# Shared-expert down product of a two-layer gated block: seven tiles in three passes of split operands, three of them behind the last expert tile, and ranks in the third chunk

## What is computed

```
t = layernorm(x)                                  # 896 tokens x 512
scores = softmax(t @ gate_w.T)                    # 16 experts
weights, indices = top_k(scores, 2)
y = sum over e of swiglu(t, w1[e], w3[e], w2[e]) * w_e      # inner width 352
z = swiglu(t, sw1, sw3, sw2)                      # shared expert, inner width 704
x = x + tanh(g_ffn[1]) * (y + z)
swiglu(t, a, b, o) = (silu(t @ a.T) * (t @ b.T)) @ o.T
```

## Time and profile before

| what | value |
|---|---|
| median of 3 runs | 979.6 us (975.99 to 981.77) |
| the profiled execution, its own time | 978.74 us |
| its span, first to last instruction | 977.1 us |
| PE busy | 939.0 us, 96% |
| DVE, ACT, POOL busy | 45%, 30%, 8% |
| chain that ended last, share of PE | 89% |
| mean granted TensorE clock | 0.987 of full |

### The profile page before, as it was taken

How to read it: one execution, slowest core, us unless ns; L and a number is a source line. 1 busy time by engine, 2 the same in 40 slices (tenths; PEclk the granted TensorE clock), 3 DMA queues, 4 the chain that set the end, 5 groups by cost and what they waited for, 6 DMA issues and landing times.

```text
span 977.1 us, 17840 instructions
## 1 busy us (share of the span) xinstructions
PE 939.0 (96%) x7481; PEld 713.2 (73%) x7482; DVE 442.6 (45%) x747; ACT 291.5 (30%) x466; POOL 74.8 (8%) x110
## 2 busy tenths in 40 slices
PE   5999999999999999989999999999999999999991
PEld 5878787878888787779999445887896455655550
DVE  6664544545445457862220353796344122222224
ACT  4633333333333334642221121335310022222210
POOL 0000000000000003000000000021005102222211
PEclk9999999999999999989999999999999999999996
DMA  8000010000101011052000302900604318977726
GB/s 335 33 2 33 2 33 2 33 27 9 76 1 34 1 62 49 2 204 120 1 1 3 126 1 68 399 27 17 250 1 153 120 33 301 327 246 247 259 72 224
DMA packets 26773, 96.04 MB, mean 98 GB/s; under 512 B 3282, under 2 KB 4306, under 8 KB 23634
## 3 DMA queue, kind: packets, MB, share of 16 engines
q1 hardware_dynamic: 20354, 72.69, 21.0%
q0 software_dynamic: 6352, 22.35, 6.1%
HBM read 76.37 MB, written 18.66 MB: 97 GB/s over the span
## 4 chain that ended last, share of the span: by engine, by line
PE 89%; DVE 5%; ACT 3%; DMA 2%; issue 1%; SPq 0%; POOL 0%; POOLq 0%; DVEq 0%; ACTq 0%
PE ps L554 18%; PE ps L555 16%; PE ps L556 16%; PE ps L971 10%; PE ps L818 7%; PE ps L981 5%; PE ps L634 4%; PE ps L945 4%; PE ps L617 3%; PE ps L840 1%; PE ps L656 1%; PE ps L962 1%; PE ps L603 1%; PE ps L988 1%; DMA token_rows<-arena,to_row 1%
## 5 line engine op out<-in xcount | busy, mean ns | idle before, releaser
L554 PE MATMUL ps<-arena_r 128*125 128x512 f32 (+1 forms) x416 | 164.1, 395 | 2.9 <-DVE arena_r L1322 2.9
L555 PE MATMUL ps<-arena_r 128*125 128x512 f32 (+1 forms) x416 | 157.2, 378 | 0.0
L556 PE MATMUL ps<-arena_r 128*125 128x512 f32 (+1 forms) x416 | 157.0, 377 | 0.0
L554 PE MATMUL ps<-hT,arena_r 128*128 128x448 f32 (+1 forms) x368 | 136.2, 370 | 2.4 <-DVE arena_r L1341 1.1
L556 PE MATMUL ps<-hT,arena_r 128*128 128x448 f32 (+1 forms) x368 | 134.4, 365 | 0.0
L555 PE MATMUL ps<-hT,arena_r 128*128 128x448 f32 (+1 forms) x368 | 134.4, 365 | 0.0
L971 PE MATMUL ps<-arena 128*128 x336 | 102.9, 459 | 0.0
L1037 ACT ACTIVATE arena<-arena,mbias,mscale 125x448 f32<-125x448 f32 x96 | 66.2, 752 | 101.9 <-DVE arena L1449 101.9
L554 PEld LDWEIGHTS ps<-arena_r 128*125 128x125 f32 (+1 forms) x416 | 78.2, 188 | 20.5 <-issue 3.9
L556 PEld LDWEIGHTS ps<-arena_r 128*125 128x125 f32 (+1 forms) x416 | 78.1, 188 | 13.8
L555 PEld LDWEIGHTS ps<-arena_r 128*125 128x125 f32 (+1 forms) x416 | 78.3, 188 | 10.8
(11 more groups left out here) (208 smaller groups left out, 1119.7 us busy)
## 6 DMA issues: line engine op xcount, KB each, us to landing
arena<-in_e SPq DMA_DIRECT2D x16, 1408.0 KB, 6.6
arena<-in_e SPq DMA_DIRECT2D x16, 512.0 KB, 7.5
sorted_rows<-arena POOLq DMA_DIRECT2D x1, 7453.0 KB, 33.4
land_c<-in_ctx SPq DMA_DIRECT2D x8, 752.0 KB, 4.3
arena<-sorted_rows POOLq DMA_DIRECT2D x21, 257.0 KB, 5.6
land_w<-in_gu SPq DMA_DIRECT2D x8, 512.0 KB, 5.1
arena<-token_rows SPq DMA_DIRECT2D x14, 256.0 KB, 4.4
arena<-in_e SPq DMA_DIRECT2D x16, 192.0 KB, 9.1
```

The source lines that it names most:

```text
L554: mm(into, a[0], w[0], start=i == 0, stop=False)
L555: mm(into, a[0], w[1], start=False, stop=False)
L556: last = mm(into, a[1], w[0], start=False, stop=i == len(operands) - 1)
```

## The change

`BEFORE = 4` token tiles of the shared down product stay ahead of or within the first expert tile (tile 3 in two halves), and tiles 4, 5 and 6 go behind the last expert product. Each tile is formed by three fp32r matmuls per chunk in place of one plain one. For that `sh2` and `hsh[m]` are split: ACT copies the high halves, DVE subtracts the low ones (`shared_low`). ACT also keeps copies of `sh2` high and of part of the low half of chunk 4 for the late tiles, because their first places lie in expert slots. Slot 2 is loaded only when tile 3 is done. The rank matmuls move from ahead of chunk 4 into chunk 2, before its last product; on DVE the tables follow at once, and `shared_hidden(2)` to `(5)` come behind them. POOL may scatter the first choice once `dest_set` is 1, and reads its loop counts before it waits for the last scatter. On DVE the late tiles' `shared_out` stands in the last loop, between the adds of j=1.

```diff
@@ memory
-        sh2 = at(37120, 6, D)
-        hsh = [at(31744 + m * TOK, TOK) for m in range(6)]
+        sh2 = halves(19440, 37120, landing("land_2", 37120, 6 * D), 6, D)
+        A_HL = [A_SH + m * 1024 for m in range(4)] + [22512, A_HT]
...
+        hsh = [halves(31744 + m * TOK, A_HL[m], land_h[m], TOK) for m in range(6)]
+        sh2_kept = at_r(896, 6, D)
+        h4_kept = at_r(3968, TOK - BEFORE * P)
...
-        A_XR = A_SH
+        A_XR = 45824
...
-        SHARED_BANK = (4, 5, 0, 1, 0, 1, 0)
+        SHARED_BANK = (4, 5, 0, 1, 0, 1, 2)
@@ SP
-            for e in range(NSLOT):
-                if e == NSLOT - 1:
-                    sp.wait_ge(ff_mm, MC + 6)
-                load_expert(e)
+            load_expert(0)
+            load_expert(1)
+            sp.wait_ge(ff_mm, MC + 6)
+            load_expert(3)
...
             post(1)
+            sp.wait_ge(sh_copied, 9)
+            sp.wait_ge(y_mm, 3 * NT + BEFORE)
+            load_expert(2)
@@ PE
-                if m == 4:
-                    pe.wait_ge(both_set, 1)
-                    pe.wait_ge(tri_set, 4)
-                    mm(ps[:, 6, 0:RT], lower, both.rearrange("p t e -> p (t e)"), start=True, stop=True)
-                    mm(ps[:, 7, 0:RT], ones, both.rearrange("p t e -> p (t e)"), start=True, stop=True
-                       ).then_inc(rank_mm, 1)
                 gate_up(m, sh13[m], size, 0, 0)
                 gate_up(m, sh13[m], size, 1, 0)
-                if m == 4:
+                if m == 3:
                     pe.wait_ge(rank_sv, 2)
                 gate_up(m, sh13[m], size, 0, 1)
+                if m == 2:
+                    pe.wait_ge(ff_h, MC + 2)
+                    pe.wait_ge(chosen, 2)
+                    pe.wait_ge(tri_set, 4)
+                    mm(ps[:, 2, 0:RT], lower, both.rearrange("p t e -> p (t e)"), start=True, stop=True)
+                    mm(ps[:, 3, 0:RT], ones, both.rearrange("p t e -> p (t e)"), start=True, stop=True
+                       ).then_inc(rank_mm, 1)
                 gate_up(m, sh13[m], size, 1, 1).then_inc(ff_mm, 1)
...
+            def shared_part(t, first, end):
+                if first == 0 and t >= 2:
                     pe.wait_ge(y_sv, 3 * NT + t - 1)
...
+                for m in range(first, end):
+                    z = SH_CHUNKS[m]
+                    if t == 0:
+                        pe.wait_ge(hsh_low, m + 1)
...
+                    mm(into, h[0], w[0], start=m == 0, stop=False)
+                    mm(into, h[0], w[1], start=False, stop=False)
+                    last = mm(into, h[1], w[0], start=False, stop=m == 5)
...
-            for t in range(5):
-                shared_down(t)
+            for t in range(BEFORE - 1):
+                shared_part(t, 0, 6)
...
             rows_T(0)
-            shared_down(5)
+            shared_part(BEFORE - 1, 0, 3)
             up_expert(0)
             rows_T(1)
-            shared_down(6)
+            shared_part(BEFORE - 1, 3, 6)
             hidden_T(0)
...
             hidden_T(last1)
+            pe.wait_ge(sh_copied, 9)
+            shared_part(BEFORE, 0, 1)
             down_expert(last1)
+            shared_part(BEFORE, 1, 6)
+            for t in range(BEFORE + 1, NT):
+                shared_part(t, 0, 6)
@@ ACT
+            act.wait_ge(sh_ld, 32)
+            fn(sh2[0][:, 0:4], sh2[2][:, 0:4], ACT.Copy)
+            fn(sh2[0][0:96, 4:6], sh2[2][0:96, 4:6], ACT.Copy).then_inc(w_high, 1)
...
+                if m == 2:
+                    act.wait_ge(rank_mm, 1)
+                    for bank, counted in ((2, place_), (3, tmp16)):
+                        fn(counted.rearrange("p t e -> p (t e)"), ps[:, bank, 0:RT], ACT.Copy).then_inc(rank_sv, 1)
...
+                act.wait_ge(ff_h, MC + m + 1)
+                fn(hsh[m][0][0:size], hsh[m][2][0:size], ACT.Copy).then_inc(sh_copied, 1)
+
+            fn(sh2_kept[:, 0:4], sh2[0][:, 0:4].bitcast(F32), ACT.Copy).then_inc(sh_copied, 1)
+            fn(sh2_kept[0:96, 4:6], sh2[0][0:96, 4:6].bitcast(F32), ACT.Copy).then_inc(sh_copied, 1)
+            act.wait_ge(hsh_low, 5)
+            fn(h4_kept[0:96], hsh[4][1][0:96, BEFORE * P:TOK].bitcast(F32), ACT.Copy).then_inc(sh_copied, 1)
@@ DVE, ranks
             for t in range(NT):
-                then(v.tensor_tensor(place_[:, t, :], place_[:, t, :], cnt, ALU.add))
+                v.tensor_tensor(place_[:, t, :], place_[:, t, :], cnt, ALU.add)
                 then(v.tensor_tensor(cnt, cnt, tmp16[:, t, :], ALU.add))
@@ DVE, the last loop
             for t in range(NT):
+                if t >= BEFORE:
+                    shared_out(t)
                 dve.wait_ge(back_ld[t][1], 16)
...
                 v.tensor_tensor(x[:, t, :], x[:, t, :], back[t][1], ALU.add).then_inc(out_st, 1)
@@ POOL
-            pool.wait_ge(dest_set, 2)
...
+                pool.wait_ge(dest_set, j + 1)
...
-            pool.wait_ge(scattered, 16 * 2 * NT)
             pool.wait_ge(tables_set, 1)
             last3, last2, last1, tiles = counts(pool)
+            pool.wait_ge(scattered, 16 * 2 * NT)
+            pool.wait_ge(ff_h, MC + 6)
```

More of the change, by code:

```diff
@@ L52 @@
 ROW = D + 2
+BEFORE = 4
 LN_EPS = 1e-5
@@ L237, in flamingo @@
         xgT = at(47616, KC, P)
-        A_XR = A_SH
-        yr = at(A_SH + 2 * ROW, D)
-        A_TO = A_SH + 2 * ROW + D
+        A_XR = 45824
+        yr = at(A_XR + 2 * ROW, D)
+        A_TO = A_XR + 2 * ROW + D
         weight = at(A_TO + 8, 1)
-        back = [[at(31744 + (2 * t + j) * D, D) for j in range(2)] for t in range(NT)]
+        back = [[at(28144 + t * D, D), at(4352 + t * D if t < 5 else 44288 + (t - 5) * D, D)] for t in range(NT)]
         lgT = at(9800, TOK, rows_=2 * NE)
@@ L408, in counts @@
                     for i in range(4)]
-        WEIGHTS = ("wk0a", "wk0b", "wv0", "wkv1a", "wkv1b", "gate", "wo0", "wq1", "wg1", "wo1")
+        WEIGHTS = ("wk0a", "wk0b", "wv0", "wkv1a", "wkv1b", "gate", "wo0", "wq1", "wg1", "wo1", "sh2")
         def nth(name):
@@ L934, in _ @@
                 gate_up(m, sh13[m], size, 1, 1).then_inc(ff_mm, 1)
             pe.wait_ge(ff_h, MC + 5)
-            pe.wait_ge(sh_ld, 32)
-            def shared_down(t):
-                if t >= 2:
+            pe.wait_ge(w_low, nth("sh2"))
+            def shared_part(t, first, end):
+                if first == 0 and t >= 2:
                     pe.wait_ge(y_sv, 3 * NT + t - 1)
-                for m, z in enumerate(SH_CHUNKS):
-                    if t == 0 and m == 5:
-                        pe.wait_ge(ff_h, MC + 6)
-                    last = mm(ps[:, SHARED_BANK[t], :], hsh[m][0:z, t * P:(t + 1) * P], sh2[0:z, m, :],
-                              start=m == 0, stop=m == 5)
-                last.then_inc(y_mm, 1)
@@ L949, in _ @@
-            for t in range(5):
-                shared_down(t)
+                into = ps[:, SHARED_BANK[t], :]
+                for m in range(first, end):
+                    z = SH_CHUNKS[m]
+                    if t == 0:
+                        pe.wait_ge(hsh_low, m + 1)
+                    h, w = ([half[0:z, t * P:(t + 1) * P] for half in hsh[m][:2]],
+                            [half[0:z, m, :] for half in sh2[:2]])
+                    if t >= BEFORE:
+                        w[0] = sh2_kept[0:z, m, :]
+                        if m == 4:
+                            h[1] = h4_kept[0:z, (t - BEFORE) * P:(t - BEFORE + 1) * P]
+                    mm(into, h[0], w[0], start=m == 0, stop=False)
+                    mm(into, h[0], w[1], start=False, stop=False)
+                    last = mm(into, h[1], w[0], start=False, stop=m == 5)
@@ L952, in _ @@
+                if end == 6:
+                    last.then_inc(y_mm, 1)
+            for t in range(BEFORE - 1):
+                shared_part(t, 0, 6)
             pe.wait_ge(tables_set, 1)
@@ L1660, in _, with shared_low @@
             feed_low(MC + 1, sh13[1])
+            dve.wait_ge(w_high, nth("sh2"))
+            v.tensor_tensor(sh2[1][:, 0:4], sh2[2][:, 0:4], sh2[0][:, 0:4].bitcast(F32), ALU.subtract)
+            v.tensor_tensor(sh2[1][0:96, 4:6], sh2[2][0:96, 4:6], sh2[0][0:96, 4:6].bitcast(F32), ALU.subtract
+                            ).then_inc(w_low, 1)
             def shared_hidden(m):
-                hidden(MC + m, m, SH_CHUNKS[m], 1.0, silu1[m % 2], hsh[m])
+                hidden(MC + m, m, SH_CHUNKS[m], 1.0, silu1[m % 2], hsh[m][2])
+            def shared_low(m):
+                z = SH_CHUNKS[m]
+                dve.wait_ge(sh_copied, m + 1)
+                v.tensor_tensor(hsh[m][1][0:z], hsh[m][2][0:z], hsh[m][0][0:z].bitcast(F32), ALU.subtract
+                                ).then_inc(hsh_low, 1)
             dve.wait_ge(lg_mm, 3)
@@ L1682, in _ @@
             shared_hidden(1)
+            shared_low(0)
             then(v.tensor_copy(idxf, idx8[:, :, 0:2]))
@@ L1733, in _ @@
             v.tensor_copy(tile_expert[:], texpf).then_inc(tables_set, 1)
+            shared_hidden(2)
+            shared_low(1)
```

(19 more changed lines are left out.)

42 lines of the change are left out of this document (19 added, 23 removed).

## The result

| | before | after |
|---|---|---|
| median of 4 runs | 977.8 us (975.92 to 981.77) | 963.66 us (962.99 to 964.5) |
| ratio of the times, 95% interval | | 0.985 (0.983 to 0.987) |
| profiled execution, own time | 978.74 us | 964.5 us |
| its span | 977.1 us | 962.8 us |

The two spans differ by 14.3 us, and three stretches hold it: ahead of the last `down_expert` (954.10 in the earlier trace rows, 935.92 now) -18.2 us; from there to the start of the last addition (18.06 before, 23.81 now) +5.75; from there to the end of the span (4.94 and 3.07) -1.9.

What follows compares the result with a forecast made beforehand. PE was taken as the bound, working 96% of the span and idle for 20 us in the tail. Front -18.4 us (-19.7 + 1.25) and tail +5.5 gave -12.9, so 979.6 became 966.7 us, range 963 to 971.

Steps and rivals of the forecast that it cites:

- Cheaper tiles: Ahead of the expert loop, four tiles in passes at 4.10 us replace seven plain ones at 5.15 us: -19.7 us.
- Stall in tile 0: At tile 0's last three matmuls PE waits for the low half of chunk 5: +1.25 us (0.8 to 2).
- Ranks and tables: Rank counts copied 12.5 us earlier, tables at 727.5; first sorted tile in place at 759.5, before PE at 763.1: hidden.
- My rival for that case: First sorted tile no earlier than 771.1: PE idles 8 us, loses 2.5 more by half clock; chance 0.06.
- Expert 2's weights: Slot 2, asked for at about 772.8, lands at 783, before its first use at 789.3: hidden by 6 us.
- The tail: Behind the last expert product, tile 6 waits 6.5 us for tile 4's `shared_out`, then runs partly at half clock: +5.5 us.
- the last store: At the end, the last store runs alone and takes 0.4 us (0 to 0.9) less than 4.25 us.
- The rule on the clock: A PE pause halves the clock and the next burst starts cold: tail +5.5 us by it, +3.1 without.
- Tile 6 is no burden: Rival in the tail: clock does not fall or tile 3's rows land early; +3.1 or less, 964.3 to 963; chance 0.13.
- PE's own loads show: Rival: PE's reads of counts and each tile's expert cost 0 to 3 us, giving 968 to 971; chance 0.14.
- The ranks bring nothing: Rival at the first sorted tile: it comes no earlier than 771.1, PE idles 8 us, 977.2 us; chance 0.06.
- Slower: Rival: slot 2 filled late, each us beyond 789.3 paid in full, gain gone at 10.5 us late; chance 0.02.

Runs made afterwards that it cites:

- ranks late: Changed kernel with the rank matmuls back ahead of chunk 4 and hidden 2 and 3 back ahead of the tables; 972.57 us, ratio 0.994 to before.
- plain tiles: Changed kernel with plain down products in place of three passes, no splits, slot 2 loaded at once; 969.42 us, ratio 0.991 to before.
- clock kept: Changed kernel with 28 more fp32r matmuls into an unused bank between tiles 5 and 6, keeping PE busy; 962.99 us, ratio 0.984 to before.
- tile 6 free: Changed kernel with tile 6 on PE no longer waiting for tile 4's `shared_out`; 960.56 us, ratio 0.981 to before.
- passes none late: Changed kernel with all seven tiles in passes ahead of or within the first expert tile (`BEFORE = 7`); 972.43 us, ratio 0.995 to before.
- outs early: As tile 6 free, with `shared_out` of tiles 4 and 5 ahead of the additions j=1, tile 6's at t = 4; 961.03 us, ratio 0.980 to before.
- four late tiles: As outs early, with `BEFORE = 3` (tiles 3 to 6 late) and own banks for tiles 5 and 6; 955.87 us, ratio 0.978 to before.

## Why the prediction came out as it did

**Cheaper tiles: right, with a small miss in the pace.** The passes start 0.233 us apart for 0.228 predicted, so a tile takes 4.19 us for 4.10. The four tiles in front took 0.4 us more than the sum said.

**Stall in tile 0: right in place, smaller.** PE waits for the low half of chunk 5 from its 16th matmul on, 0.8 us against 1.25 priced; the slower pace took part of it. The two misses nearly cancel, which is luck, and the front is -18.2 us for -18.4 (-18.0 by the ruler).

**Ranks and tables: right.** Counts copied at 718.09 (717.9), tables at 727.5 (727.5), hidden 2 at 728.5 (728.6), no wait of PE at chunk 4. In place was the tile at 759.3 (759.5), but by other terms: the load took 758.65 - 752.54 = 6.1 us to arrive, where I had 3.1 from the earlier trace rows, and what I had put on ACT's copies and the count loads did not come on top, so the right time is luck too. (By its own rate, 0.84 us for 768 columns, the sum for ACT's 3456 copied columns should have been 3.8 us, not 3.5; the rows show 3.3, and nothing hung on it.) The load was hidden either way. That the early ranks carry the gain is shown by the run without them: 9.2 us. My rival for that case had 10.5.

**Expert 2's weights: right.** Asked for at 773.3 (772.8), and PE never waits for them.

**The tail: the mechanism right, two terms off, the last store most.** The wait of tile 6 was 6.54 us (6.5), released by tile 4's `shared_out` as forecast. Behind it the matmuls ran at half pace for seven or eight of the 18, not twelve, so tile 6 took 6.0 us for 6.5 (the 5 us at half pace that I took from the earlier trace rows were 3.4 here, but 5.2 in ranks late and 5.8 in plain tiles), and the last addition came 5.75 us later than before for 5.9. The term that failed is the last store: I took 0.4 us off the 4.25 us between the end of the last addition and the end of the span, and it was 962.8 - 960.42 = 2.4 us, so 1.9 off. My own bound for it was 0.9. What the store meets at the transfers differs. Stretches of before, with the last addition ending at 972.85:

```profile
970.00:973.00 3.00, 0.00 (x0) 0.00 (x0) 1.95 (x3) 0.00 (x0) 0.00 (x0) 0.50 1.04 396
973.00:977.00 4.00, 0.00 (x0) 0.00 (x0) 0.00 (x0) 0.00 (x0) 0.00 (x0) 0.50 0.69 266
```

There the last three additions come in one burst of 1.95 us, behind the last loads back, and the share stays at 1.05 up to 975, two us after the last of them: the stores stand in line. After the change the last addition ends 5.3 us behind the one before it, and its store finds the transfers idle (a share of 0.01 in the last stretch above). The other kernels agree. The time from the end of the last addition to the end of the span is 2.4 us where that addition comes alone (clock kept, plain tiles, ranks late), 2.6 with 1.5 us between the additions (tile 6 free), and 4.2 to 4.3 where three end in one burst right behind the loads (passes none late, outs early). With four late tiles three also end in one burst, but the transfers had run empty just before (a share of 0.00 from 950 to 951), and it is 2.6. So it is the queue and not the burst that counts. This term, 1.5 us beyond the 0.4 that I took off, is half of the 3.0 us by which the time was missed, and nearly all of the 1.4 us between the predicted change, -12.9 us, and that of the two profiled executions, -14.3. The other half is no step of mine: the median of the kernel before fell by 1.8 us with its fourth run.

**The rule on the clock.** I had weighed tail sums of +5.5 and +3.1 us by whether the clock falls in the pause. It fell, and the run that kept PE at work over the pause shows its price as 1.6 us of tile 6. The Trainium skill, "TensorE: Matmul & The Clock Gate", section "HAM oscillation", describes this case (a pause of PE, and the next burst starts cold), and the trace agrees: 0.43 us a matmul behind the pause, 0.23 a little later.

**Rivals.** *Tile 6 is no burden* had the band 963 to 964.3, and the measured 963.66 lies in it; by the number alone one would take it for true. The traces refute it: the clock fell, tile 3's rows landed no earlier, and tile 6 was late. The time came so low by the last store and the lower median of before. Without the wait, in tile 6 free, the tile is indeed no burden, and the whole tail is back at 22.8 us. *PE's own loads show*: no wait or gap appears ahead of the expert tiles. *The ranks bring nothing*: the first sorted tile was in place 4.1 us early. *Slower* needed a late slot 2, which never was late.

## What to carry to other kernels

Moving work of the critical engine into a pause at the end pays only if what it uncovers at the front is ready; here (with the passes in each) late tiles without early ranks gave 5 us, early ranks with no tile late also 5, and both together 14. The passes alone were priced at 6.0 us, so neither move by itself shows any gain beyond them; a kernel with only the passes was not run. Once that cover is known in us, it can be used up: one more tile brought 4 us in front for 1 us in the tail, and the next fix in the same place brought nothing. In a tail, look at each wait of the moved work for the bank that it could use instead, since a wait there costs itself and a slow clock behind it; and price the last store by how crowded the transfers are at that moment, not by what it took before.
